# Post-norm transformer layer on one core: when a token group's last statistics and normalisation run

## The reference, cut to what matters

```python
qkv = x @ Wqkv.T + b                      # q: 16 heads of 32; k, v: one head of 32
attn = softmax(causal(q k^T / sqrt(32)))
x = layernorm(x + (attn v) @ out_w.T + out_b)
x = layernorm(x + sum over top 2 experts of score * (silu(x w1) * (x w3)) w2)
```

## Time and profile before

| what | value |
|---|---|
| median of 3 runs | 1181.79 us (1181.24 to 1182.4) |
| profiled execution, its own time | 1181.34 us |
| its span, first to last instruction | 1179.2 us |
| busy: TensorE / VectorE / ScalarE / GpSimd | 93% / 75% / 60% / 14% |
| mean granted TensorE clock | 0.978 of full |

### The profile page before, as it was taken

The page is one execution under the profiler, slowest core; times in us unless marked ns, Lnnn a source line. Parts: engine busy times, 40 slices in busy tenths (PEclk is TensorE's granted clock), DMA queues, the critical chain, the costliest instruction groups (busy, mean ns, idle before and its releaser), DMA issues.

```text
span 1179.2 us, 18318 instructions
## 1 busy us (share of the span) xinstructions
PE 1094.8 (93%) x6056; PEld 524.9 (45%) x6080; DVE 890.2 (75%) x1095; ACT 712.2 (60%) x828; POOL 165.4 (14%) x153
## 2 busy tenths in 40 slices
PE   5499999998999999999989998999999999999976
PEld 4146433743335543333734743374333564333442
DVE  3176688769888689889667767885988867988956
ACT  5354568337885477888327347844778546788811
POOL 2250121102001012001004103020200101200000
PEclk9599999999999999999999999999999999999998
DMA  3992540164001532000164164016210143200000
GB/s 125 206 150 67 117 103 1 37 144 108 1 1 38 112 104 36 2 2 1 45 136 110 45 135 108 1 38 143 86 23 1 37 87 94 36 1 1 2 2 36
DMA packets 65677, 74.36 MB, mean 63 GB/s; under 512 B 14224, under 2 KB 48016, under 8 KB 65552
## 3 DMA queue, kind: packets, MB, share of 16 engines
q1 hardware_dynamic: 49968, 58.74, 19.6%
q0 software_dynamic: 13584, 11.54, 6.6%
q10 hardware_dynamic: 2000, 2.51, 0.7%
HBM read 25.58 MB, written 8.39 MB: 29 GB/s over the span
## 4 chain that ended last, share of the span: by engine, by line
PE 70%; DVE 16%; issue 6%; POOL 2%; ACT 2%; SPq 2%; DMA 1%; DVEq 0%; ACTq 0%; POOLq 0%
PE sc L1059 18%; PE bank L1081 16%; PE sc L949 9%; DVE psum_k L749 8%; PE sc L1198 7%; PE bank L949 7%; PE sc L1213 2%; PE sc L1099 2%; SPq L364 2%; PE bank L1099 2%; POOL prob L460 2%; ACT prob L583 1%; DVE stats L825 1%; PE sc L1147 1%; PE bank L1206 1%
## 5 line engine op out<-in xcount | busy, mean ns | idle before, releaser
L583 ACT ACTIVATE prob<-sc 128x1024 f32<-128x1024 f32 x544 | 525.1, 1026 | 158.5 <-PE sc L1059 145.4
L749 DVE TENSOR_TENSOR psum_k<-psum_k,prob 128x2048 f32<-128x2048 f32 x170 | 395.6, 2327 | 5.1
L1059 PE MATMUL sc<-q_st,k_st 128*128 128x512 f32 x1088 | 334.9, 429 | 33.2 <-DMA q_st<-q_lo 13.1
L1059 PEld LDWEIGHTS sc<-q_st,k_st 128*128 128x128 f32 x1088 | 186.7, 191 | 280.8 <-ACT prob L583 178.0
L1081 PE MATMUL bank<-prob,v_sb 128*32 128x512 f32 x2176 | 290.2, 610 | 0.0
L460 POOL TENSOR_SCALAR_AFFINE_SELECT prob<-prob 128x1024 f32<-128x1024 f32 x64 | 88.0, 1410 | 596.0 <-ACT prob L583 596.0
L1198 PE MATMUL sc<-prob,w_sb 128*128 128x512 bf16 x488 | 117.5, 380 | 5.1 <-DVE prob L898 2.9
L749 DVE TENSOR_TENSOR psum_k<-prob 128x2048 f32<-128x2048 f32 x28 | 64.1, 2290 | 55.0 <-ACT prob L583 42.0
L1081 PEld LDWEIGHTS bank<-prob,v_sb 128*32 128x32 f32 x2176 | 44.0, 108 | 106.6 <-issue 90.8
L949 PE MATMUL bank<-q_st,wq_hi 128*128 128x512 f32 x240 | 80.8, 401 | 0.0
L615 ACT ACTIVATE prob<-sc 128x512 f32<-128x512 f32 x64 | 37.3, 597 | 68.1 <-PE sc L1198 68.0
(11 more groups left out here) (127 smaller groups left out, 1003.6 us busy)
## 6 DMA issues: line engine op xcount, KB each, us to landing
q_st<-q_hi SPq DMA_DIRECT2D x128, 128.0 KB, 2.7
q_st<-q_lo SPq DMA_DIRECT2D x128, 128.0 KB, 2.7
res<-in_x SPq DMA_DIRECT2D x8, 1024.0 KB, 5.1
res<-ob_sb POOLq DMA_DIRECT2D x8, 1024.0 KB, 8.1
out_x<-res SPq DMA_DIRECT2D x32, 256.0 KB, 2.5
res<-in_xT SPq DMA_DIRECT2D x7, 1024.0 KB, 5.3
w_sb<-in_w POOLq DMA_DIRECT2D x8, 256.0 KB, 10.9
prob<-in_wqkvT ACTq DMA_DIRECT2D x4, 288.0 KB, 5.8
```

The costliest lines, as they stand in the source:

```text
L583: nc.scalar.activation(prob[t % NP][:, half * HW:(half + 1) * HW], score_half(q // TB, 2 * t + half).rearrange("p m n -> p (m n)"), ACT.Ex ...
L749: nc.vector.tensor_tensor(acc[:, :], first[:, :], prob[t % NP][:, :], ALU.add).then_inc(add_v, 1)
L1059: last = nc.tensor.matmul(dst, k_st[:, k * P:(k + 1) * P], q_st[slot][:, c * HJ:(c + 1) * HJ, at:at + P], start=True, stop=not shift)
```

## The change

VectorE's four residual additions of group g-1's expert output stay ahead of group g. The statistics move to the tile at which group g's first query block has its context scaled (its last tile + 3), and the normalisation to two tiles later, each behind what VectorE does at that tile. GpSimd's `make_rstd` moves from behind the first block's mask to behind the second's, in front of `add_bias`. Between passes over b, and at the very end, additions, statistics and normalisation still follow one another. So the order differs at six places: groups 1, 2 and 3 in each of two passes.

```diff
--- before.py
+++ after.py
@@ -490,9 +490,9 @@
                 for g in range(NG):
                     for q in range(TB * g, TB * (g + 1)):
                         mask(q)
-                        if q == TB * g and g:
-                            make_rstd(2 * g)
                         if q == TB * g + 1:
+                            if g:
+                                make_rstd(2 * g)
                             add_bias(g)
                         if q < 3:
                             load_experts(q)
@@ -819,10 +819,11 @@
 
                 def residual(g, t, src, done):
                     r = res[g % 2][:, t, :]
-                    ins = nc.vector.tensor_tensor(r, src, r, ALU.add)
-                    ins.then_inc(done, 1)
+                    nc.vector.tensor_tensor(r, src, r, ALU.add).then_inc(done, 1)
+
+                def measure(g, t, done):
                     dve.wait_ge(done, count(b, done, TB * g + t + 1))
-                    step(nc.vector.bn_stats(stats[:, t, :], r))
+                    step(nc.vector.bn_stats(stats[:, t, :], res[g % 2][:, t, :]))
                     return nc.vector.bn_aggr(mv[:, t, :], stats[:, t, :])
 
                 def normalise(g, n, done):
@@ -841,7 +842,8 @@
                         dve.wait_ge(outproj, count(b, outproj, TB * g + t + 1))
                         if t == 0:
                             dve.wait_ge(biased, count(b, biased, 16 * (g + 1)))
-                        last = residual(g, t, LOW[t], resid1)
+                        residual(g, t, LOW[t], resid1)
+                        last = measure(g, t, resid1)
                     last.then_inc(mv_ready, 1)
                     with if_more(dve, b, g):
                         split_low_q(b, g + 1, 0)
@@ -911,17 +913,20 @@
                             with if_more(dve, b, g):
                                 judge(b, g + 1)
 
-                def finish_experts(g):
+                def add_experts(g):
                     for t in range(TB):
                         dve.wait_ge(down_done, count(b, down_done, TB * g + t + 1))
-                        last = residual(g, t, down_bank(g, t), resid2)
+                        residual(g, t, down_bank(g, t), resid2)
+
+                def measure_experts(g):
+                    for t in range(TB):
+                        last = measure(g, t, resid2)
                     last.then_inc(mv_ready, 1)
-                    normalise(g, 2 * g + 2, out_ready)
 
                 for g in range(NG):
                     guard(g)
                     if g:
-                        finish_experts(g - 1)
+                        add_experts(g - 1)
                     t0, t1 = FIRST[TB * g], LAST[TB * g + TB - 1]
                     for t in range(t0, t1 + 1):
                         if t > t1 - 2:
@@ -931,13 +936,19 @@
                         for q in denominators_at(t):
                             if q >= TB * g:
                                 normalise_context(q)
+                        if g and t == LAST[TB * g] + DLAG:
+                            measure_experts(g - 1)
+                        if g and t == LAST[TB * g] + DLAG + 2:
+                            normalise(g - 1, 2 * g, out_ready)
                     split_low_context(g, 2)
                     normalise_context(TB * (g + 1) - 1)
                     split_low_context(g, 3)
                     finish_attention(g)
                     route(g)
                     experts(g)
-                finish_experts(NG - 1)
+                add_experts(NG - 1)
+                measure_experts(NG - 1)
+                normalise(NG - 1, 2 * NG, out_ready)
                 assert steps[0] == V_STEPS, steps[0]
 
         @block.tensor
```

## The result

The changed kernel takes **1202.53 us** (median of 4, 1197.58 to 1203.17) against 1182.1 for the kernel before, run beside it: 1.016 times as long, 95% interval 1.014 to 1.0181. The forecast was 1187.5, range 1176.5 to 1191. "Slower" was right; the loss of 20.4 is three and a half times the 5.7 forecast. The profiled execution is one of the short ones: 1197.58, span 1195.5, mean granted clock 0.973. Its span is 16.3 longer than the 1179.2 of before.

What follows compares the result with a forecast made beforehand. TensorE was taken as the bound (70% of the chain, VectorE 16%). Groups 1, 2, 3 added 1.05 + 1.2 + 0.6 = 2.85 per pass, 5.7 for two, on 1181.34: 1187.0, median 0.45 above, so 1187.5; range 1176.5 to 1191.

Steps and rivals of the forecast that it cites:

- T1 of group 2: Start of VectorE's transposition of group 2's first denominators, from the group's first residual; the slot's 3.6 loss there goes.
- VectorE without idle time: Sign: VectorE never idles from the first add, at tile 1's exponentials, to the second block's denominators.
- T2: Start of VectorE's transposition of a group's second denominators, from its first residual; scores behind it shift +1.2 in group 2.
- Nothing is removed but the rstd wait, whose two GpSimd instructions now run beside adds: Start of each group: VectorE's rstd wait of 1.58 goes; make_rstd, 1.3 on GpSimd, was costed at nothing outside group 1.
- I take 1.55: Group 2, second block: GpSimd's mask of tile 19 holds VectorE's adds, 0.78 per mask half, 1.55 in all.
- 168.0 + 1.84 + 1.55: Group 1, second block: normalisation 1.84 after add 9, plus 1.55 hold by tile 11's mask, ends at 171.4.
- The clock, 1.55 in group 1: TensorE, idle 4.4 before group 1's second-block scores, then runs at half clock: 1.55 lost, making group 1 +1.05.
- The rival that it falls in group 2 too: Half clock also follows the 3.8 TensorE idle in group 2: 1.55 more per pass, 1190.6; chance 0.07.
- The same 3.9 + 1.84 come back in the next query block: Each group's second block: VectorE still does statistics, 3.9, and normalisation, 1.84, before those denominators.
- the cover shrank: Group 2, first block: VectorE idled 1.7 and 2.2 waiting for exponentials, work time it doesn't get back.
- the waits only change place: Rival: second-block times lie within 1.2 of the old and errors cancel: 1181.8, give or take 2; chance 0.19.
- The mask holds nothing: Rival: adds and masks hardly meet or don't exclude one another, so 1.55 goes from each group: 1177.5; chance 0.24.

Runs made afterwards that it cites:

- The shift of one tile: Changed kernel with the normalisation one tile later, three instead of two tiles behind the statistics: 1196.79 us.
- small masks: GpSimd's causal masks shrunk to 8 columns of one head per half of a diagonal tile: changed kernel 1187.85 us, kernel before 1171.19 us.
- the kernel with nothing moved behind adds: Against the kernel before, all four residuals, then all statistics, then normalisation, still in front of the next group and at pass ends: 1189.37 us.
- The kernel with fillers: Changed kernel plus 32 zero-weight TensorE matmuls in group 1, before the scores that wait for the second denominators' slot: 1201.74 us.

## Why the prediction was right in direction and wrong in size

**Right: the first block's loss goes and comes back at the second.** T1 of group 2 was forecast at 289.7 behind 261.14, which is 28.6; it is 28.60. Denominators there start without a wait, and those of the second block wait. Adds start right at tile 1's exponentials (forecast 5.6 behind the first residual, measured 5.71), and the two pauses of VectorE (forecast 1.7 and 2.2) measure 1.91 and 2.11, though the mask ends the second, not exponentials. Of the other signs, "VectorE without idle time" up to the second block failed (0.93 and 0.94 for rstd), and the mask pairs were 2.68, 5.06 and 5.06 in groups 1 to 3. TensorE's new waits are 5.75 in group 1, 3.08 and 1.11 in group 2, and 1.32 in group 3, where 2 to 4 was named.

**The sum, beside the measured lengths.** The forecast was 2.85 per pass. The groups of the first pass grew by 2.85 + 2.06 + 1.05 = 5.96, those of the second by 4.21 + 1.74 + 1.24 = 7.19; with group 0's 1.3 and the end's 1.84 that is the 16.3 of the spans. Of the 10.6 above the forecast's 5.7, T2 has 3.2 in the first pass (40.75, 57.62 and 73.06 where the forecast had 38.9, 56.9 and 72.4) and 3.0 in the second, the pass ends have 3.2, and the clock has 1.2 beyond its two times 1.55. Added up, these are the 10.6; that lateness at T2 is length lost one for one is taken, not shown. By steps:

- *"Nothing is removed but the rstd wait, whose two GpSimd instructions now run beside adds", at no cost.* Failed. GpSimd in group 1 of the changed kernel (group 2 has 2.19 and 3.06); VectorE waits 0.93 and 0.94 for them in the two groups:

```profile
162.89 2.19 POOL L485 TENSOR_SCALAR rstd<-mv 128x4 f32<-128x4 f32 x1 [11.89 <-DVE mv L827]
165.16 3.05 POOL L487 TENSOR_TENSOR rstd<-rstd,mhalf 128x4 f32<-128x4 f32 x1
168.18 1.40 POOL L477 DMA_DIRECT2D res<-ob_sb  x1
169.07 2.68 POOL L460 TENSOR_SCALAR_AFFINE_SELECT prob<-prob 128x1024 f32<-128x1024 f32 x2
```

  and the same two in the kernel before, where VectorE stands idle for them:

```profile
267.99 0.23 POOL L485 TENSOR_SCALAR rstd<-mv 128x4 f32<-128x4 f32 x1 [5.03 <-DVE mv L826]
268.30 1.04 POOL L487 TENSOR_TENSOR rstd<-rstd,mhalf 128x4 f32<-128x4 f32 x1
```

  Beside adds they take 5.3 instead of 1.3, longer than the two adds (4.62) that were to cover them. The shift of one tile (1196.79) confirms it: without the wait T2 is 4.7 earlier over four groups, and the median is about 5 lower. I had applied the lock to masks and not to these. By the rule of the Trainium skill (SBUF — State Buffer, "SBUF: two separate sides") a GpSimd instruction of 0.23 waits for the whole add. The trace agrees on GpSimd's side, with 2.19 and 3.05 beside adds of 2.3; on the adds themselves no hold shows (two in 4.62).
- *The mask, "I take 1.55".* Right in size in group 2 (10.80 against 9.28), and it belongs in T2. But it is no cause of the difference, as "now VectorE adds without a pause" made it: the kernel before pays as much on its way to T2 (1.57 in group 2). My T2 of group 2, 56.91, lacked the 0.94 and is 0.7 short of the measured 57.62.
- *Group 1, "168.0 + 1.84 + 1.55".* Mis-sized. VectorE there:

```profile
168.24 5.16 DVE L833 TENSOR_SCALAR res<-res,mv,rstd 128x512 f32<-128x512 f32 x4 [0.93 <-POOL rstd L487]
...
177.85 0.71 DVE L798 STREAM_TRANSPOSE rden<-sc 128x512 f32<-128x512 f32 x1
```

  The normalisation takes 5.16, not 3.39. The first of its four instructions alone lasts 3.79, past the end of both mask halves (169.07 + 2.68), which follow rstd and the bias DMA without a gap. With small masks and the same DMA all four take 2.08, and with the mask pair but no DMA 3.49 (only the normalisation moved). So the hold needs the masks; why it is longer behind the DMA isn't shown. T2 is 40.75 where I had 38.9, and where the kernel before had 39.41. With the rstd wait this is the largest miss in the sum.
- *The clock, 1.55 in group 1.* Measured 1.66 and 2.68. The rival that it falls in group 2 too didn't come: behind 3.08 and 1.11 of idle time the scores at 322.36 take 1.20.
- *Left out: the pass ends.* That the order differs "at six places" overlooked that additions and statistics come apart at the pass ends too, where no add is behind them. 1.84 at the very end is shown; about 4 in all by the medians, less surely.
- *"The same 3.9 + 1.84 come back in the next query block."* This held (the statistics take 3.76 there, 295.06 to 298.82), and "the cover shrank" counted the pauses, so it isn't a miss in the sum. It is the largest part of the slowdown in group 2, and I didn't draw the conclusion: in the front the statistics filled pauses, and leaving them there costs 1.02 in group 2. By the idle times for equal work (5.43 before, 7.31 changed, 3.39 with only the normalisation moved) that is 2.95 of the 3.92 between the last two kernels. With statistics and rstd left in place the same move of the normalisation gains 15.6.

The rival "the waits only change place" (1181.8) had T2 within 1.2 of the old ones; they are 1.3 to 2.0 later. "The mask holds nothing" falls at its premise, since the mask holds four adds for 1.5; and with no mask to speak of, the change is still 16.7 slower.

**What stays open.** The profiled executions of the changed kernel (1197.58 and 1198.38) are 3 to 7 shorter than its other six (1201.59 to 1204.5). So of about 20 lost, 16.3 are placed by the profile, and some 4 are in executions that have none. Where rstd is made was never tried by itself with the statistics in front, nor the statistics' place with rstd made early.

## What to carry to other kernels

Before work is moved away from a front, see what the next instruction would wait for anyway: work that fills such a pause is nearly free where it is (1.02 of 3.9 here), and costs its full length where the engine has no pause. Here moving only the step that waits for another engine, with time for its input to be ready, took 1.3% off, where moving everything added 1.6%. Price a moved step at its new neighbours, the small instructions of the other engine included, and compare an engine's idle time over the whole stretch, for equal work, rather than single waits.

## What the runs showed of the hardware that was not expected

- Two GpSimd instructions of 128x4 elements, 0.23 and 1.04 long alone, take 2.19 and 3.06 beside VectorE's adds, while those keep their pace (two in 4.62). The normalisation, in contrast, was held by GpSimd's masks: 5.16 for four instead of 1.91, and 2.08 with the small masks. One of the four took 3.79.
- In some executions TensorE pauses for 2.05 to 2.69 at the end of group 3 with no wait that the profile shows; in the kernel before it is 0.72 and 0.77. Of seven such pauses in five of the profiles, three were followed by a granted clock of 0.66 over 5 us, and four by 1.00. From the kernel with nothing moved behind adds, TensorE and its window:

```profile
559.60 2.93 PE L1108 MATMUL bank<-prob,ones 128*32 128x512 f32 x16 [2.08 <-issue]
```

```profile
560.00:565.00 5.00, 5.00 (x28) 1.67 (x21) 1.70 (x3) 0.00 (x0) 0.40 (x1) 0.66 0.61 211
```

  The kernel with fillers has a pause of 2.69 of this kind at 1139.70, again with 0.66 behind it. What causes it wasn't tried, nor whether the executions without a profile have it. It may be one reason for the spread of some 4 us within a kernel.
